# Pooled keys convolved by three matrix products instead of five VectorE and ScalarE steps, in a two-layer kernel with a computed instruction order

## The reference, cut to what matters

```python
scores = jnp.einsum('bhqd,bhkd->bhqk', q, k) * scale
scores = scores * (1.0 + 0.5 * NORADRENALINE)
top_k = max(1, int(s * 0.2))                               # 102 of 512 keys
threshold = lax.top_k(scores, top_k)[0][..., -1:]
scores = scores * jnp.where(scores >= threshold, 1.24, 1.0)
scores_pooled = scores.mean(axis=-2)                       # mean over the queries
li = lax.conv_general_dilated(scores_pooled, conv_w, window_strides=(1,), padding=[(1, 1)],
        feature_group_count=HEADS, ...) + conv_b[None, :, None]   # 3 taps a head
scores = scores * li[:, :, None, :]
probs = jax.nn.softmax(scores, axis=-1)
```

## Time and profile before

| | us |
|---|---|
| median of 3 runs | 2884.38 |
| lowest, highest | 2880.81, 2885.79 |
| the profiled execution's own time | 2883.22 |
| its span, first to last instruction | 2882.0 |
| VectorE busy | 2227.5 |
| TensorE busy | 2172.6 |
| ScalarE busy | 1554.3 |
| POOL busy | 1204.0 |
| mean granted TensorE clock | 0.878 of full speed |

### The profile page before, as it was taken

How to read it: one execution, slowest core, us unless ns; L and a number is a source line. 1 busy time by engine, 2 the same in 40 slices (tenths; PEclk the granted TensorE clock), 3 DMA queues, 4 the chain that set the end, 5 groups by cost and what they waited for, 6 DMA issues and landing times.

```text
span 2882.0 us, 33776 instructions
## 1 busy us (share of the span) xinstructions
PE 2172.6 (75%) x8767; PEld 1113.4 (39%) x8767; DVE 2227.5 (77%) x5937; ACT 1554.3 (54%) x3331; POOL 1204.0 (42%) x1166
## 2 busy tenths in 40 slices
PE   4159777988788777978878787878779787868654
PEld 2016222553244522644244522544235532444214
DVE  5874788968898688978799787978879786952371
ACT  4316824776176823885267823876157842744423
POOL 2020253715455153724555063723445154634461
PEclk7589799988998898989989899989989799989857
DMA  4001112232043312333133312323133221313223
GB/s 108 0 22 36 24 38 84 84 101 83 27 124 72 104 52 75 97 80 93 38 102 83 102 49 69 110 68 101 31 106 95 86 65 54 104 41 112 83 80 102
DMA packets 137461, 215.13 MB, mean 75 GB/s; under 512 B 17872, under 2 KB 57440, under 8 KB 134112
## 3 DMA queue, kind: packets, MB, share of 16 engines
q1 hardware_dynamic: 133088, 203.88, 25.0%
q0 software_dynamic: 4096, 8.40, 1.0%
HBM read 190.06 MB, written 22.15 MB: 74 GB/s over the span
## 4 chain that ended last, share of the span: by engine, by line
DVE 35%; PE 16%; issue 12%; ACT 9%; POOL 6%; DVEq 3%; DMA 2%; POOLq 0%; ACTq 0%; SPq 0%
DVE ps_rest L1644 6%; DVE wmask L833 6%; DVE best L975 4%; DVEq L977 3%; DVE hg L1656 3%; ACT wmask L815 3%; PE ps_rest L1385 2%; DVE z L1143 2%; POOL slots L1800 2%; PE ps_rest L1375 2%; PE ps_rest L1831 2%; PE ps_rest L1845 1%; PE ps_rest L1471 1%; DMA cols<-slots 1%; PE ps_rest L1833 1%
## 5 line engine op out<-in xcount | busy, mean ns | idle before, releaser
L1445 POOL TENSOR_TENSOR gat<-sil,cbs 128x512 f32<-128x512 f32 x256 | 325.1, 1274 | 469.8 <-ACT sil L1410 396.6
L1410 ACT ACTIVATE sil<-ps_rest,w_b1T 128x512 f32<-128x512 f32 x256 | 175.7, 686 | 471.5 <-PE ps_rest L1385 417.4
L833 DVE TENSOR_SCALAR_CACHE_REDUCE wmask<-z,tc 128x512 bf16<-128x512 f16 x512 | 349.2, 741 | 21.3 <-ACT z L800 18.1
L1009 POOL TENSOR_SCALAR wmask<-wmask 128x512 bf16<-128x512 bf16 x256 | 158.1, 617 | 341.7 <-DVE wmask L966 337.7
L1093 PE MATMUL ps_att<-z,Vp 128*32 128x128 f32 x2048 | 269.6, 277 | 16.8 <-DVE z L1165 16.8
L1385 PE MATMUL ps_rest<-rest_hT,WF 128*128 128x512 f32 x512 | 279.9, 633 | 0.0
L1375 PE MATMUL ps_rest<-gat,WP 128*128 128x512 f32 x512 | 268.7, 608 | 14.4 <-POOL gat L1445 14.4
L766 PE MATMUL ps_att<-qk 128*128 128x512 bf16 x512 | 222.6, 452 | 45.6 <-DMA qk<-bounce 21.6
L1093 PEld LDWEIGHTS ps_att<-z,Vp 128*32 128x32 f32 x2048 | 202.5, 110 | 131.3 <-issue 93.4
L1697 POOL TENSOR_TENSOR rest_c<-rest_c,hg 128x512 f32<-128x512 f32 x128 | 162.5, 1270 | 130.0 <-DVE hg L1656 129.9
L1684 POOL TENSOR_TENSOR gat<-cols,cbs 128x512 f32<-128x512 f32 x128 | 163.5, 1278 | 123.2 <-DVE cols L1565 123.2
(11 more groups left out here) (361 smaller groups left out, 4824.5 us busy)
## 6 DMA issues: line engine op xcount, KB each, us to landing
cbs<-spreads SPq DMA_DIRECT2D x128, 256.0 KB, 3.7
ccs<-spreads SPq DMA_DIRECT2D x128, 256.0 KB, 3.4
WF<-in_w SPq DMA_DIRECT2D x64, 256.0 KB, 2.7
WP<-in_w SPq DMA_DIRECT2D x64, 256.0 KB, 2.6
WF<-in_wfc SPq DMA_DIRECT2D x64, 256.0 KB, 2.7
WG<-in_wgate SPq DMA_DIRECT2D x64, 256.0 KB, 3.0
WP<-in_wproj SPq DMA_DIRECT2D x64, 256.0 KB, 3.0
qk<-bounce SPq DMA_DIRECT2D x32, 384.0 KB, 5.2
```

Of the source, the lines that this page charges most:

```text
L833: od.up(dve.tensor_scalar(wmask[:, i, :], z_at[i], tc[:, 0, i:i + 1], None, ALU.is_ge, ALU.add, accum_out=tc[:, 1, i:i + 1]))
L1445: weighed0.up(pool.tensor_tensor(gat[m % 2], sil[m % 2], cbs[e % 2][:], ALU.mult))
```

## The change

- The three tap factors are multiplied into `ones_block` once, at the start of the rest branch, which gives three matrices `spread_tap[:, a]` (VectorE, three instructions of 128x128).
- The four multiplications of the choice write straight into the middle of `pool_pad` instead of `att.c[2]`. The copy L1039 goes.
- TensorE does three products, with `pool_pad` shifted by 0, 1 and 2 columns, which add up in one bank. It waits for the four multiplications itself.
- ScalarE's copy L1030 and VectorE's three tap instructions go. One VectorE instruction reads the bank, adds the bias and multiplies with K.
- `Wo`, needed once at the start, is loaded into a buffer that is free then, to make room.
- Planned durations, all places of `TIMETABLE`, `PERIOD` and `NEAR` are new.

```diff
-PERIOD = -65.7
+PERIOD = -65.1
 TIMETABLE = {
-    "pe_rest": (155.6425, (4063.8, 2909.1, 2381.5, 1586.6)),
+    "pe_rest": (155.6425, (3802.0, 2960.8, 2457.6, 1743.9)),
...
+    wts["Wo"] = rest.c[1][:, 0:P]
...
+    spread_tap = sb("spread_tap", [P, 3, P])
...
-    pooled, pool_ps, padded = sig("pooled"), sig("pool_ps"), sig("padded")
+    taps, pool_ps = sig("taps", 3), sig("pool_ps")
...
     def dve_late():
+        for a in range(3):
+            taps.up(dve.tensor_scalar(spread_tap[:, a], ones_block[:], wts["attn_cw"][:, a:a + 1], None, ALU.mult))
+        yield 0.6
...
-                keyed.up(dve.tensor_tensor(att.c[2][ch, :], KT[ch, :], sums[ch, :], ALU.mult))
+                keyed.up(dve.tensor_tensor(pool_pad[ch, 1:S + 1], KT[ch, :], sums[ch, :], ALU.mult))
...
     def pe_rescale(b):
-        yield pooled.at(b)
-        pe.wait_ge(*pooled.at(b))
-        pool_ps.up(pe.matmul(att.bank[0][:], ones_block[:], att.c[0][:], start=True, stop=True))
-        yield 1.09
-
-    def act_rescale(b):
-        yield pool_ps.at(b)
-        act.wait_ge(*pool_ps.at(b))
-        padded.up(act.activation(pool_pad[:, 1:S + 1], att.bank[0][:], ACT.Copy))
-        yield 0.64
+        yield taps.all(0)
+        pe.wait_ge(*taps.all(0))
+        for g in range(GROUPS):
+            yield keyed.at(b, g)
+            pe.wait_ge(*keyed.at(b, g))
+        for a in range(3):
+            mm = pe.matmul(att.bank[0][:], spread_tap[:, a], pool_pad[:, a:a + S], start=a == 0, stop=a == 2)
+        pool_ps.up(mm)
+        yield 1.83
 
     def dve_rescale(b):
         c0, c1, c2 = att.c
-        cw = wts["attn_cw"]
-        for g in range(GROUPS):
-            yield keyed.at(b, g)
-            dve.wait_ge(*keyed.at(b, g))
-        pooled.up(dve.tensor_copy(c0[:], c2[:]))
-        yield 0.46
         yield bounced.at(b, 5)
         dve.wait_ge(*bounced.at(b, 5))
-        yield padded.at(b)
-        dve.wait_ge(*padded.at(b))
-        od.settle()
-        od.up(dve.tensor_scalar(c0[:], pool_pad[:, 0:S], cw[:, 0:1], wts["attn_cb"][:], ALU.mult, ALU.add)); od.settle()
-        yield 0.59
-        od.up(dve.scalar_tensor_tensor(c1[:], pool_pad[:, 1:S + 1], cw[:, 1:2], c0[:], ALU.mult, ALU.add)); od.settle()
+        yield pool_ps.at(b)
+        dve.wait_ge(*pool_ps.at(b))
+        od.up(dve.scalar_tensor_tensor(c1[:], att.bank[0][:], wts["attn_cb"][:], KT[:], ALU.add, ALU.mult)); od.settle()
         yield 0.79
-        od.up(dve.scalar_tensor_tensor(c2[:], pool_pad[:, 2:S + 2], cw[:, 2:3], c1[:], ALU.mult, ALU.add)); od.settle()
-        yield 0.79
-        od.up(dve.tensor_tensor(c1[:], KT[:], c2[:], ALU.mult)); od.settle()
-        yield 0.73
         dve_split(c1[:], parts, c0[:], splitted)
...
-            yield from act_rescale(b)
...
-    NEAR = 0.152
+    NEAR = 0.155
```

More of the change, by code:

```diff
@@ new lines @@
+    "pe_rest": (155.6425, (3802.0, 2960.8, 2457.6, 1743.9)),
+    "act_rest": (84.0600, (5379.2, 4869.1, 4597.9, 5501.7)),
+    "dve_rest": (96.7100, (3773.8, 6716.3, 6241.2, 5268.9)),
+    "pool_rest": (113.9225, (1269.3, 2236.8, 2604.7, 1900.6)),
+    "sp_rest": (15.3000, (6869.3, 5260.9, 5242.4, 5904.2)),
+    "pe_mixtures": (10.3100, (4903.7, 5395.6, 3858.3, 3210.4)),
+    "act_mixtures": (6.3000, (7222.3, 5469.3, 4558.1, 7644.8)),
+    "dve_mixtures": (13.5500, (5191.3, 4707.7, 5936.7, 7586.7)),
@@ new lines @@
+    "pool_mixtures": (3.9300, (9297.5, 10218.0, 12727.2, 14584.4)),
+    "dve_finishes": (4.9600, (5965.5, 3350.0, 2149.6, 4374.2)),
+    "pool_finishes": (9.0400, (4003.0, 5314.8, 5582.7, 4300.3)),
+    "sp_finishes": (0.9000, (7426.2, 10390.7, 11481.1, 10734.2)),
+    "pe_choices": (42.2400, (1918.7, 1679.7, 2708.3, 2804.1)),
+    "act_choices": (2.5600, (9752.0, 10467.3, 8864.4, 4434.8)),
+    "dve_choices": (58.8100, (4346.7, 4551.5, 5163.4, 3733.2)),
+    "pool_choices": (20.4800, (8256.7, 8070.6, 7985.6, 9964.9)),
@@ new lines @@
+    "pe_attention": (58.2100, (7745.9, 4877.8, 3670.2, 3872.1)),
+    "act_attention": (76.1800, (9970.4, 8368.9, 8897.6, 14234.6)),
+    "dve_attention": (98.4700, (8027.1, 6946.6, 6166.6, 6186.2)),
+    "pool_attention": (6.5463, (5849.9, 5351.1, 6023.1, 5831.0)),
+    "sp_attention": (10.3500, (11444.6, 8888.3, 9166.0, 7450.6)),
+    "pe_prepares": (8.9150, (5657.8, 5851.2, 6036.6, 5717.6)),
+    "act_prepares": (3.9500, (2617.2, 3135.0, 2576.8, 0.0)),
+    "dve_prepares": (13.8550, (9989.4, 12083.4, 12646.2, 11576.5)),
@@ L80 @@
+    "pe_refills": (12.8000, (6911.0, 5914.2, 6046.6, 7116.3)),
+    "act_refills": (19.2000, (6406.4, 8184.4, 7232.8, 5870.2)),
+    "sp_rows": (0.3937, (10695.5, 10039.8, 8947.8, 10143.1)),
+    "sp_ups": (10.6875, (7381.0, 7610.7, 8281.2, 8410.7)),
+    "sp_downs": (7.0875, (8728.5, 7297.9, 5371.9, 2951.5)),
 }
@@ L168, in emit @@
              ("dt_b", [P, DC]), ("out_projT", [P, DC, D]))
-    wts = {n: sb("w_" + n, shape) for n, shape in EARLY + LATER}
+    wts = {n: sb("w_" + n, shape) for n, shape in EARLY + LATER if n != "Wo"}
     loaded, late = sig("loaded", len(EARLY) + 1, 16), sig("late", len(LATER), 16, 30.0)
```

28 lines of the change are left out of this document (removed).

## The result

The changed kernel takes 2917.9 us (median of 4 runs, 2914.8 to 2920.9), the kernel before beside it 2882.6 us (4 runs, 2880.7 to 2885.8). The ratio is 1.0122, with a 95% interval of 1.0110 to 1.0135: 1.2% slower. The forecast of 2845 us and its range, 2826 to 2872, were wrong, in sign too.

A forecast was written before the change was run, and what follows sets the result against it. The prediction took VectorE, busiest at 77% of the span, with its waits as the bound. Terms of 21.9 (arrangement), 16.9 (work) and 1 (batch 0) summed to 39.8 us less: 2845 us forecast, range 2826 to 2872.

The forecast's parts named there:

- The arrangement: Order of experts0 around the choice: batches 4 to 7 come down to A's 324.6 us, 21.9 us less.
- A: Arrangement without a tail of experts0 behind the choice (batches 1 to 3 before); 324.6 us a batch, expected everywhere.
- Three more counts: Search: 64 counts behind experts1 instead of 61, 2 us a batch, but moved, not added; taken as 0.
- VectorE's work: Rescale instructions on VectorE: net 2.4 us less a batch; taken as 16.9 us for batches 1 to 7.
- The path behind the choice: Last mask to softmax: norm chain some 3.5 us earlier, added products hidden; gain between 0 and 4.5 us a batch.
- B: Arrangement with seven steps of experts0 as tail behind the choice (batches 4 to 7 before); 1320.3 us together.
- R3: Rival: three products on TensorE act as a barrier, each batch 5.8 us longer; 2903 us, chance 0.08.
- Batch 0: First batch, its rescale bare with no second branch beside it: 1 us gain, ends -2 and 2.
- the last stretch: Last batch's rest branch, 326 us from 2556 to the end, alone in both kernels: 0.
- R1: Rival: only the work is gained; the tail's wait comes back elsewhere; 19 us gain, 2865 us, chance 0.18.
- R2: Rival: TensorE's clock falls between choice and softmax, both projections slower, 24 us lost; 2869 us, chance 0.07.

The follow-up runs named there:

- e3: Code of the kernel before, with the order of its own batch 2 repeated for batches 3 to 7; 2858.4 us, ratio 0.9918.
- e2: Code of the kernel before, with its instructions in the changed kernel's order; 2913.7 us, ratio 1.0109.
- e12: e9 with VectorE's additions of the gathered expert rows behind count 16 of the search's fourth round instead of count 1, batches 2 to 6; 2895.6 us.
- e4: Changed code in the order of batch 2 of the kernel before, repeated for batches 3 to 7; 2856.3 us, ratio 0.9913.
- e14: e11 with VectorE's additions of the gathered rows behind the 16th count instead of the eighth, batches 2 to 7; 2836.5 us, ratio 0.9823.
- e16: Code of the kernel before in the order of e14; 2837.6 us, ratio 0.9838.
- e9: Changed kernel with the search's first VectorE update kept together and ScalarE's second- and third-round signs (search counts) placed as in A; 2918.2 us.
- e11: e4 with two fewer ScalarE steps of experts0 ahead of the search's third-round signs (ScalarE counts), batches 2 to 7; 2867.0 us.
- e13: Changed kernel with only VectorE's additions of the gathered rows moved behind the fourth round's count 16, batches 2 to 6; 2918.0 us.

## Why the prediction was wrong, step by step

- *The arrangement (21.9 us), "That is A everywhere": the step that failed.* That A brings 22 us is right (e3: 22 to 24). That the changed kernel's order is A was not: the old code in that order takes 2913.7 us (e2). I had compared one mark, experts0 ahead of or behind the choice. The new order differs from A in places that I did not look at. On VectorE the additions of the gathered rows stand behind count 1 of the last round instead of count 8. On ScalarE the signs of the second and third round stand four and two expert steps later. Undoing this pair gave 22 us (e12), about a third of the 62 us between the changed kernel and the new code in A (e4). The new order also has the experts later: their results are stored at 76.8 us in its batch 5, at 74.6 in batch 3 of e4.
- *"Three more counts", taken as 0: the wrong question.* I priced how many counts stand behind experts1, not which instruction between them waits for a DMA. The search of batch 5 is 8.8 us longer than that of A in e4.
- *VectorE's work (16.9 us): failed as a gain, its bound of 0 was right.* The count of work is right: the instructions of the rescale sum to 19 us less over 8 batches. By the page VectorE's busy time fell by 6.9 us only (2227.5 to 2220.6); 8.0 us of the difference are the 24 `tc<-tc` of the updates, which took 14.3 us instead of 6.3. "The softmax's start is set elsewhere, and VectorE's saved time turns into idle time" was the lower end, and it is what happened (e3 and e4, e14 and e16).
- *The path behind the choice: half right.* The products are 2.7 to 2.9 us long in batches 1 to 6, against 2.6 estimated. The third window of the changed kernel's batches 1 to 6 is 26.7 to 31.8 us, against 29.8 to 31.0 in A and 42.4 in B, so the tail's wait went as forecast. L1043 waits for the products 1.5 to 2.9 us in these batches, where some 1.5 was forecast. The transposes of Mamba's norm start right at the products' end in batches 1 to 3 (791.20 with the products ending at 791.36), so the count by which the products end 0.6 us before the transposes' input was wrong there, and right in batches 5 and 6. R3's sign is there, without R3's price.
- *Batch 0 and the last stretch.* Batch 0, forecast 1 us shorter, is 0.7 longer (289.0 against 288.3), inside its bounds. The last stretch, put at 0, is 7.8 us shorter. The prediction's lower end is also some 3 us too low for its own terms: 21.9 + 31.5 + 2 us less than 2884.4 is 2829, not 2826.
- *R1*, that the tail's wait comes back elsewhere, was the nearest rival, and its warning ("the new order is not A to the letter") was right. It stopped at no gain; in batch 5 the search took back 10.7 us of the 13.6 given, and softmax and projection 7.4. Of these 7.4 us 4.6 are in A too; the cause of the other 2.8 was not tested.
- *R2, the clock*, showed its sign but not its price. The eight records that took 3.70 us in batches 2, 4, 5 and 6 before took 5.9 to 6.7 in batches 2 to 5 of the changed kernel and 3.70 only in batch 6. In batch 5 they ran at a granted clock of 0.55, in batch 6 at 1.00. But Mamba's projection ahead of them, also eight records, went the other way: 3.60 us in batch 5, 5.29 in batch 6. Over batches 1 to 7 the two projections add up to 70.2 us against 68.7 before, so the lower level moved from one to the other, and 1.6 us are left where R2 had 24. The Trainium skill (TensorE: Matmul & The Clock Gate, "Why this matters for your kernels") advises against idle gaps between bursts of matmuls; the trace agrees in kind, with gaps of 1.95, 1.87 and 1.12 us in TensorE's work ahead of the slow eight of batch 5.

Left open are the 39 us between e12 and e4. Of these, 13 are batch 7's search (142.8 us against 129.8), in which the additions were not moved and which is 3.4 us longer than even in the changed kernel. Some 20 are the searches of batches 2 to 6, where the experts are still later and TensorE waits for weights; that these two are the cause was not tested. What in the new table delays the experts' results by 2.2 us was not taken apart.

## What to carry to other kernels

When a change comes with a new computed order, the order can be the larger change: run the old code in the new order and the new code in the old one before crediting the code. To compare two orders, walk each engine's list for instructions that wait on a DMA or another engine and count what is queued behind them; a mark such as "no tail behind the choice" says nothing about the rest. If taking one wait away brings nothing, look in the new trace for the wait that took its place and remove both before calling it harmless.

## What was not expected

- Where VectorE waited for the gathers (e9, e11), the additions started 2.6 to 2.8 us after the last gather's issue. In the changed kernel they started 3.2 us after it without a wait, so the trace before an experiment showed nothing of how near the next limit was.
- An addition on VectorE that takes 0.34 us takes up to 1.36 when it starts during a step of GpSimd's; the eight together took from 3.6 us (e13) to 6.0 (e11), by their place.
- A store that waits for VectorE held up weight loads queued behind it on SyncE, and TensorE for 6.3 to 6.8 us (e13).
- The pair of moves on the A order gave 2836.5 us, 1.6 to 1.8% under the kernel before, with either code.
